# Idle products at the start, small loads on ScalarE's queue, and a last batch in three units

## The reference

```python
x = x + (x @ W.T + (x @ A0[label]) @ B0.T * 0.5)         # layer 0, rank 32
x = x + quantise(x, thresholds, deltas, zero_points)     # layer 1, 8 levels of scale
x = x + x @ W2[adapter].T                                # layer 2, weights of 1024 x 1024 per batch
x = x + (x @ B3[adapter].T) @ A3[adapter].T              # layer 3, rank 16
```

## Time and profile before

| | |
|---|---|
| median of 3 runs | 486.47 us (485.25 to 486.58) |
| the profiled execution: its time, its span | 486.57 us, 484.8 us |
| TensorE, matmul records: busy | 462.4 us, 95% |
| VectorE: busy | 427.1 us, 88% |
| ScalarE: busy | 315.0 us, 65% |
| mean granted TensorE clock | 0.988 |

### The profile page before, as it was taken

The page is one execution under the profiler, slowest core; times in us unless marked ns, Lnnn a source line. Parts: engine busy times, 40 slices in busy tenths (PEclk is TensorE's granted clock), DMA queues, the critical chain, the costliest instruction groups (busy, mean ns, idle before and its releaser), DMA issues.

```text
span 484.8 us, 7178 instructions
## 1 busy us (share of the span) xinstructions
PE 462.4 (95%) x2944; PEld 424.8 (88%) x2944; DVE 427.1 (88%) x389; ACT 315.0 (65%) x237; POOL 11.0 (2%) x16
## 2 busy tenths in 40 slices
PE   3998997999999999999999999999999999997995
PEld 3998996889998899989998999989998899884883
DVE  3589999999899977999599997999869996899953
ACT  4489979955696529956297635986269641966600
POOL 0001000000000000000000000000000010000000
PEclk9999999899999999999999999999999999997999
DMA  7883030264025442073323642135123332246022
GB/s 254 315 315 99 3 99 0 87 235 160 12 78 187 171 126 87 1 272 110 103 89 126 233 124 88 39 136 175 39 87 122 139 126 88 87 166 221 0 88 87
DMA packets 17461, 60.25 MB, mean 124 GB/s; under 512 B 2964, under 2 KB 5012, under 8 KB 13332
## 3 DMA queue, kind: packets, MB, share of 16 engines
q1 hardware_dynamic: 17428, 59.79, 35.9%
HBM read 51.39 MB, written 8.39 MB: 123 GB/s over the span
## 4 chain that ended last, share of the span: by engine, by line
PE 74%; DVE 15%; issue 6%; ACT 3%; DMA 1%; SPq 0%; DVEq 0%; ACTq 0%
PE l_ps L759 32%; PE l_ps L708 28%; PE l_ps L774 6%; DVE quant L578 5%; DVE cand L552 3%; PE bx_ps L791 3%; PE bx_ps L730 2%; PE l_ps L804 1%; DVE quant L572 1%; DMA x_raw<-x 1%; ACT cand L391 1%; DVE x_lo L505 1%; DVE cand L560 1%; PE l_ps L718 1%; DVE w_lo L487 1%
## 5 line engine op out<-in xcount | busy, mean ns | idle before, releaser
L759 PE MATMUL l_ps<-x,w_sb 128*128 128x256 f32 x896 | 197.4, 382 | 2.3 <-DVE x L632 2.0
L759 PEld LDWEIGHTS l_ps<-x,w_sb 128*128 128x128 f32 x896 | 170.6, 192 | 25.8 <-issue 2.9
L578 DVE COPY_PREDICATED quant<-mask,cand 128x2048 f32<-128x2048 int8 (+3 forms) x70 | 143.9, 2055 | 12.0 <-ACT mask L401 7.1
L401 ACT ACTIVATE mask<-magnitude,thr_bias 128x2048 fp8e5<-128x2048 f32 (+3 forms) x70 | 115.8, 1655 | 38.2 <-DVE quant L578 38.0
L391 ACT ACTIVATE cand<-x,inv_delta 128x2048 f32<-128x2048 f32 (+3 forms) x80 | 132.1, 1652 | 4.5 <-DVE quant L572 1.8
L552 DVE TENSOR_SCALAR cand<-cand,delta 128x2048 f32<-128x2048 f32 (+3 forms) x80 | 86.2, 1077 | 12.2 <-ACT cand L391 12.0
L708 PE MATMUL l_ps<-x_hi,w_hi 128*128 128x256 f32 x512 | 86.0, 291 | 9.7 <-ACT w_hi L325 7.4
L560 DVE TENSOR_SCALAR cand<-cand,lower,upper 128x2048 f32<-128x2048 f32 (+3 forms) x80 | 91.3, 1142 | 0.4
L708 PE MATMUL l_ps<-x_lo,w_hi 128*128 128x256 f32 x512 | 83.8, 287 | 0.0
L708 PE MATMUL l_ps<-x_hi,w_lo 128*128 128x256 f32 x512 | 83.7, 286 | 0.0
L708 PEld LDWEIGHTS l_ps<-x_hi,w_hi 128*128 128x128 f32 x512 | 72.2, 195 | 12.8 <-ACT w_hi L325 7.4
(11 more groups left out here) (52 smaller groups left out, 234.8 us busy)
## 6 DMA issues: line engine op xcount, KB each, us to landing
w_sb<-w SPq DMA_DIRECT2D x31, 1024.0 KB, 5.1
out<-x SPq DMA_DIRECT2D x32, 256.0 KB, 2.2
x_raw<-x SPq DMA_DIRECT2D x15, 512.0 KB, 5.7
w_sb<-w SPq DMA_DIRECT2D x7, 512.0 KB, 6.2
a_raw<-a SPq DMA_DIRECT2D x48, 64.0 KB, 4.4
a_raw<-a SPq DMA_DIRECT2D x8, 128.0 KB, 4.6
x<-w SPq DMA_DIRECT2D x1, 1024.0 KB, 5.6
x_raw<-x SPq DMA_DIRECT2D x2, 256.0 KB, 4.7
```

The source lines that it names most:

```text
L401: act.activation(mask[:, m % MASKS, 0:n], magnitude[:, 0:n], ACT.Relu, bias=thr_bias[:, k:k + 1], scale=STEEP, saturate=False).then_inc(ma ...
L578: dve.copy_predicated(y, mask[:, m % MASKS, 0:n].bitcast(I8), t).then_inc(merged, 1)
L759: last = nc.tensor.matmul(l2_bank(b, q)[:, i * S:(i + 1) * S], w2_tile(b, o)[:, k * P:(k + 1) * P], x2[:, b % SLOTS, k * S:(k + 1) * S], s ...
```

## The change

The change does three things. TensorE runs 24 products of the identity with itself, `WARM`, before its first tile, into a bank that is not yet in use. ScalarE's queue issues the loads of both id vectors and of the three parameter vectors, ahead of its other work; SyncE issues tile 3 before B0, and the orders in which ScalarE and VectorE split the weights are written out anew: ScalarE splits tiles 4 and 5 before the low-rank product's high part, and VectorE computes the parameters between `add_diag(4)` and `add_diag(5)` instead of after all splits. The last batch has three units, of blocks 0 to 3, 4 and 5, 6 and 7; the work between their steps, the parts of `last_layer2` and the place of `split_bx(B - 2)` change with them.

```diff
-LAST_SPLIT = 5
+PARTS = (0, 4, 6, 8)
+WARM = 24
 UNITS = ((0, 0, HW), (0, HW, HW)) + tuple((b, 0, BW) for b in range(1, B - 1))\
-    + ((B - 1, 0, LAST_SPLIT * S), (B - 1, LAST_SPLIT * S, BW - LAST_SPLIT * S))
+    + tuple((B - 1, first * S, (end - first) * S) for first, end in zip(PARTS, PARTS[1:]))
+LAST = len(UNITS) - len(PARTS) + 1
...
 SyncE
-            sp.dma_start(label_ids[:, :], ...)
-            sp.dma_start(adapter_ids[:, :], ...)
             load_w0(1)
             load_w0(2)
             sp.wait_ge(ids_loaded, 2 * 16)
             load_a0(0)
+            load_w0(3)
             for q in range(4):
                 sp.dma_start(a3_raw[q * QUAD:(q + 1) * QUAD, :], b0).then_inc(b0_loaded, 16)
-            (three parameter loads)
-            for n in range(3, T):
+            for n in range(4, T):
                 load_w0(n)
...
 ScalarE, between(u, j)
-                    if j == 7:
+                    if j == 7 and s + 1 < B - 1:
                         drain_l0(s + 1, 1)
-                elif u == len(UNITS) - 2:
+                elif u == LAST:
                     if j == 2:
                         split_a3(s - 1)
-                else:
-                    if j == 1:
-                        split_bx(s - 1)
+                    if j == 3:
+                        drain_l0(s, 1)
 ScalarE, main
+            (five small loads, then as before)
             split_w0(1)
+            split_w0(2)
             split_a0(0)
-            split_w0(2)
+            split_w0(3)
             act.wait_ge(b0_loaded, 4 * 16)
             act.activation(b0_split[:, :], a3_raw[:, :], ACT.Copy, scale=0.5).then_inc(b0_hi_done, 1)
-            for n in range(3, T):
-                if n == 4:
-                    low_rank_hi(0)
-                split_w0(n)
+            split_w0(4)
+            split_w0(5)
+            low_rank_hi(0)
+            split_w0(6)
+            split_w0(7)
+            act.wait_ge(param_step, 6)
             drain_l0(0, 0)
-            act.wait_ge(param_step, 6)
             for u in range(len(UNITS)):
                 quantise(u)
+            split_bx(B - 2)
             split_a3(B - 1)
             split_bx(B - 1)
...
 VectorE, between(u, j)
-                elif u == len(UNITS) - 2:
+                elif u == LAST:
                     if j == 2:
                         split_a3(s - 1)
-                    if j in (1, 3, 5, 7):
-                        drain_l2(s - 1, j // 2)
-                else:
-                    if j == 1:
-                        split_bx(s - 1)
+                    if j == 6:
+                        drain_l2(s - 1, 0)
+                elif u == LAST + 1:
+                    if j in (0, 3, 6):
+                        drain_l2(s - 1, j // 3 + 1)
 VectorE, main: the order after is
   add_diag(1) split_x(0, 1) add_diag(2) split_w0(1) split_w0(2) add_diag(3) split_a0(0)
   split_w0(3) (B0) add_diag(4) (parameters) add_diag(5) split_w0(4) low_rank_lo(0)
   add_diag(6) split_w0(5) add_diag(7) split_w0(6) split_w0(7), all units, split_bx(B - 2), finish ...
 TensorE
-            def last_layer2(half):
+            def last_layer2(part):
-                pe.wait_ge(x2_done, x2_count(b) - 1 + half)
+                pe.wait_ge(x2_done, LAST + part + 1)
...
-                        for k in (range(LAST_SPLIT), range(LAST_SPLIT, T))[half]:
+                        for k in range(PARTS[part], PARTS[part + 1]):
...
+            pe.wait_ge(ident_ready, 1)
+            for i in range(WARM):
+                nc.tensor.matmul(l3_ps[:, 0:P], ident[:, :], ident[:, :], start=True, stop=True)
...
             for q in range(4):
                 layer2(B - 2, q)
+            last_layer2(0)
             for q in range(4):
                 low_rank3(B - 2, q)
-            last_layer2(0)
+            last_layer2(1)
             for q in range(4):
                 layer3(B - 2, q)
-            last_layer2(1)
+            last_layer2(2)
```

More of the change, by code:

```diff
@@ L644, in _ @@
             split_first_w0(1)
+            add_diag(1)
             split_x(0, 1)
[L646 removed]
+            add_diag(2)
             split_w0(1)
+            split_w0(2)
+            add_diag(3)
             split_a0(0)
[L649 to L650 removed]
+            split_w0(3)
             rows = slice(QUAD, 2 * QUAD)
@@ L654, in _ @@
                                      b0_split[rows, :].bitcast(F32), ALU.mult, ALU.subtract).then_inc(b0_split_done, 1)
-            add_diag(3)
-            for n in range(3, T):
-                if n + 1 < T:
-                    add_diag(n + 1)
-                if n == 4:
-                    low_rank_lo(0)
-                split_w0(n)
+            add_diag(4)
             dve.wait_ge(params_loaded, 3 * 16)
@@ L670, in _ @@
             dve.tensor_scalar(thr_bias[:, :], sorted_thr[:, :], -STEEP, None, ALU.mult).then_inc(param_step, 1)
+            add_diag(5)
+            split_w0(4)
+            low_rank_lo(0)
+            add_diag(6)
+            split_w0(5)
+            add_diag(7)
+            split_w0(6)
+            split_w0(7)
             dve.wait_ge(param_step, 6)
@@ L761, in layer2 @@
                 last.then_inc(l2_done, 1)
-            def last_layer2(half):
+            def last_layer2(part):
                 b = B - 1
-                if half == 0:
+                if part == 0:
                     pe.wait_ge(x0_done, 2 * B)
-                pe.wait_ge(x2_done, x2_count(b) - 1 + half)
+                pe.wait_ge(x2_done, LAST + part + 1)
                 for q in range(4):
-                    if half == 0:
+                    if part == 0:
                         pe.wait_ge(w2_loaded[q], (b + 1) * 16)
@@ L777, in last_layer2 @@
                                                     start=(i == 0 and k == 0), stop=(i == 1 and k == T - 1))
-                    if half == 1:
+                    if part == len(PARTS) - 2:
                         last.then_inc(l2_done, 1)
```

14 lines of the change are left out of this document (6 added, 8 removed).

## The result

| | before | after |
|---|---|---|
| median (lowest to highest), beside each other | 485.11 us (484.32 to 486.58) | 488.21 us (487.56 to 489.73) |
| ratio of the times, 95% interval | | 1.0064 [1.0048, 1.0081] |
| profiled execution: time, span, granted clock | 486.57, 484.8, 0.988 | 489.59, 487.8, 0.980 |
| first candidate | 29.78 | 29.70 |
| layer 2 of batch 0 starts | 83.28 | 83.21 |

Forecast were 484.2 us and a range of 482.4 to 487.4; 488.21 lies outside it. Both profiled executions are some 1.4 us above their medians, so their difference, 3.0 us of span, can stand for that of the medians, 3.1. Its parts are the differences of the table's rows: nothing at the head (−0.07 where −3.9 was forecast), 1.26 us between 83 and 411, and 1.84 in the tail (1.6 was forecast; 66.77 against 64.93 us).

A forecast was written before the change was run, and what follows sets the result against it. TensorE was taken to bound most of the span, with VectorE bounding quantisation at the head. Head −3.9 us and tail +1.6 us make −2.3, so 486.5 becomes 484.2 us, range 482.4 to 487.4.

The forecast's parts named there:

- The step that failed: Head: tile 1 stays near 9.95 and tile 2 near 11.35; small packets sharing the DMA engines cost x 0.3 us.
- my bound of 0.6 us: Head: upper end of the 0 to 0.6 us allowed for small packets sharing the DMA engines with x.
- my first rival: Head: clock falls again between the first twelve products and 11.8, gap 0.4 to 2 us; 485.8 us, chance 0.2.
- The head's gain of 3.9 us: Head: first candidate starts at 25.9 instead of 29.78, 3.9 us sooner; bounds 0.5 and 4.3.
- the forecast chain of steps: TensorE's next products from 11.8, low-rank product done about 21.1, first candidate 25.9, layer 2 of batch 0 at 79.4.
- The idle products: TensorE's start: 24 products from 1.5 us, 0.12 us a record, twice that at low clock, ending between 8.3 and 10.3.
- The overrun: Rival: idle products' records exceed about 0.2 us warm, real tiles begin at 15 to 17; 486.5 to 488 us, chance 0.13.
- The stage from 83 to 411: TensorE-bound batches after quantisation: layer 2 starts at 79.4 instead of 83.28, the head's 3.9 us passing through.
- The tail: Batch 6's layer 2 onward: TensorE stands 5.4 us for the later drain, low clock costs 2.5; 1.6 us slower (0.8 to 2.5).
- the rival in which only the tail counts: Head's gain lost between 25 and 83 us to a wait now just covered, 5.4 us stall stays; 488 us, chance 0.12.
- the sum of −2.3 us: Whole kernel: head −3.9 and tail +1.6, taken from 486.5 to give 484.2 us.

The follow-up runs named there:

- parameters early on SyncE: Changed kernel with the three parameter loads on SyncE right behind x's second half, ahead of tile 1, ids staying on ScalarE; 487.44 us, ratio 1.0038 to before.
- ids on ScalarE: Changed kernel with only the three parameter loads back on SyncE behind B0, both id loads staying on ScalarE; 484.43 us, ratio 0.9972 to before.
- a mended head: Changed kernel with all five small loads on SyncE, ids after x's second half, parameters after B0, new tail kept; 484.63 us, ratio 0.9996 to before.
- The head measured alone: Kernel before with the change's head only, all small loads on SyncE, last batch in two units as before; 482.57 us, ratio 0.9944 to before.

## Why the prediction was wrong, point by point

**The step that failed** is the one on the landings: tiles 1 and 2 "both stay about there", and "the small packets share the DMA engines with x; I take 0.3 us for them, from 0 to 0.6 us". Measured, x's second half came 2.8 us later (11.45 against 8.7), tile 1 2.9 and tile 2 3.9. I had priced the small packets by the engine time that they occupied in the earlier trace rows, 1.16 of the engines for half a microsecond, "in which most of them moved". That reading was wrong. In before the three loads were issued at 11.52, 11.98 and 12.46 and landed 2.5, 2.6 and 3.3 us later, at 14.0, 14.6 and 15.8, and the windows just ahead of the one that I had taken show the engines nearly idle:

```profile
13.00:13.50 0.50, 1.00 0.29 55
13.50:14.00 0.50, 1.00 0.11 7
14.00:14.50 0.50, 1.00 0.40 45
```

Tile 3 had been issued at 12.93, right behind them. A part of this quiet may be tile 3's own start; with the parameters early on SyncE it is not, since tile 1 had been issued 2.7 us before the engines went quiet. So what small packets cost here is the time in which nothing else moves, and not only the time that they occupy. On one queue that is already above my bound of 0.6 us: 1.1 us at the candidate and 1.5 us of nearly idle engines with the parameters early on SyncE. What a second queue adds, no row of before could show. The kernel with all five on SyncE shows that the landings, and nothing else in the new head, lost the gain: one edit, and x's half is at 8.69, tile 1 at 9.94, the candidate at 26.05. The same loads on the kernel before, and nothing else, make 3.1 us.

The Trainium skill ("DMA: Bandwidth & Descriptors", Issuing engines are not separate DMA queues) says that loads issued by different engines interleave on the same 16 DMA engines, and that several issuers save issue time only. The runs agree as far as they go: with the small loads on the second queue x came 2.8 us later. No run has them on the one queue ahead of x. How much small packets on one can slow large loads on the other that section does not say.

**From there the loss is arithmetic.** TensorE's products begin at 14.42 instead of 11.8, 2.6 us, and behind 3.1 us of standing the clock was low, as in my first rival, whose gap of "0.4 to 2 us" had become 3.1: the products up to about 17 ran at 0.215 us a record. The fall was not bound to come, and it did not set the candidate alone. With the parameters early on SyncE TensorE stood 3.0 us in the same place and went on at 0.12 us a record. And in after the copies of tiles 4 and 5 ended at the same time as the low-rank product; in the two other kernels with this head ScalarE waited 0.3 and 1.15 us for it. The low-rank copy is at 25.16 where 21.1 to 21.6 was forecast, the candidate at 29.70 where it was 25.9. The head's gain of 3.9 us is 0.07. Where the landings are right, the forecast chain of steps (11.8, 21.1, 25.9, 79.4) is met within a few tenths: 11.88, 21.26, 25.81 and 79.45 with the ids on ScalarE.

**The idle products** were costed right: forecast end between 8.3 and 10.3, measured 9.9. A record was forecast at 0.12 us and at twice that at the low clock, and seven run in the window of 1.5 to 3.0 us, 0.21 each, and sixteen in that of 7.5 to 9.0, some 0.1 each: that is nearer the lower bound of 0.107 than the 0.12 taken. The weight load is hidden. The overrun, a rival at 0.13, did not come.

**The stage from 83 to 411** was forecast to move whole. It grew by 1.26 us, because the clock behind the stand of 2.0 us was low for longer (96 records in 23.90 us, before 22.64). "Even if that fall goes away, its 1.9 us are hardly won" proved right: with all small loads on SyncE there was no fall, and TensorE waited 1.4 us for the first drain instead. From layer 2 of batch 0 to the next batch's takes 58.5 us in that kernel and in before, and 59.7 in after. A short fall is covered by VectorE and costs nothing; a long one is not, and costs 1.2.

**The tail** was right in mechanism and size. The stall is 5.0 us, forecast 5.4; the drain begins 18.2 us after layer 2 of batch 6, forecast 18.6; clock 3.1 us, forecast 2.5 of 1.7 to 3.4; the whole stretch 66.77, forecast 66.5. The experiments agree within their intervals: the old tail under the same head is 2 us faster, the new one under a mended head 2.5 us slower than the old. In single executions the size depends on how soon the clock is back: this stretch takes 65.2 to 66.8 us in the seven kernels with the late drains, and 64.3 to 65.0 in the four with the old tail. A step of 512 columns takes 1.47 us, estimated at 1.45.

**The chances.** The result came out at the number of the rival in which only the tail counts (488, chance 0.12), and its mechanism, a "first transfer delayed by small packets", is what happened, though it bit ahead of 25 us and not between 25 and 83, where I had put it. A chance of 0.12 was too low for a cost whose row was taken from another queue. That the number fits as well is luck: 488 was 486.5 plus the tail's 1.6 us, the kernel before stood at 485.11 beside the new one, and of the 3.1 us between them 1.26 are the longer fall of the clock, which I had not forecast.

With the landings mended the sum of −2.3 us (a ratio of 0.9953) stands against 0.9972 [0.9953, 0.9991] with the ids on ScalarE and 0.9996 [0.9976, 1.0016] with all on SyncE. So even there the forecast was too good by 0.9 and 2.1 us; the first interval just reaches it, the second does not. The head measured alone gives 2.7 us (1.7 to 3.8) of the 3.9, and the tail takes 2 to 2.5 where 1.6 was forecast.

## What to carry to other kernels

A load is not free because it is small: three loads of 4 KB in 432 small packets on a second queue, beside the first large loads, delayed those by 2.8 us and cost the kernel 3.1; in this kernel they belong behind the large ones that the start waits for, on the same queue. Their price is read from the time in which the engines move nothing else, and a cost taken from a row with one queue is no bound for two. A drain that frees a bank is placed by when TensorE comes back for it: five microseconds of standing cost eight here (6.6 where the clock was back sooner), because the clock falls behind the stand, and two steps earlier it costs nothing. Keeping the clock high at the start is worth what waits for TensorE there, and only if the data come before it stands again.

## What the runs showed of the hardware

**Small packets leave the engines partly idle, on one queue and on two.** With the parameters' 32-byte packets ahead of tile 1 on the one queue, the share is 0.16 and the rate 28 GB/s for 1.5 us. In 4 to 8 us the rate is 216 GB/s at a share of 0.66 with the parameters on the second queue, and 389 at 1.02 with all on one. When the second queue starts late, its own 4 KB loads take 8.4 to 10.7 us; on the one queue they took between 2.5 and 7.8. Why the engines stand while large loads are waiting is open. The one-queue kernel shows that it needs no second queue; whether the larger delay with two comes from the turns between queues or from the place ahead of x, no run here tells.

**The clock falls for different lengths after the same stand.** Layer 2 of batch 0 always follows a stand of 2.0 us. Two kernels show no fall behind it (all on SyncE; ids on ScalarE), before and four others a short one (first 96 records 22.64 us), after and seven others a longer one (23.80 to 23.93). Here is the kernel with all small loads on SyncE, and then after, in windows of TensorE:

```profile
82.00:84.00 2.00, 2.00 (x11) 1.00 0.00 0
84.00:86.00 2.00, 2.00 (x11) 1.00 0.00 0
```

```profile
83.00:84.00 1.00, 0.79 (x2) 0.50 0.00 0
...
88.00:89.00 1.00, 1.00 (x4) 0.50 0.00 0
89.00:90.00 1.00, 1.00 (x6) 0.91 0.00 0
```

The tail's stall shows it too: the 64 records behind it take 15.5 and 15.7 us in two kernels and 16.7 to 17.0 in the five others that have it. Each of the two makes 1.1 to 1.6 us, where single executions of one kernel differ by 0.7 to 4.5 us here; that the one causes the other is likely, since profiled executions alone show the clock, but not shown. What decides the length, or whether there is a fall at all, was not found: in the head a stand of 3.0 us was followed by none in one kernel, and stands of 2.9, 3.1 and 3.6 us by a low clock in three.

**The granted clock reads 1.00 at the very start whatever the rate.** In after the column says 1.00 for 1.5 to 3.0 us, where the idle products' records take 0.21 us, and for 7.5 to 9.0, where they take some 0.1. From the first fall on (0.50 in 15 to 16) it agrees with the pitch. Until the column has shown its first fall, the distance between starts is the measure, and not the column.

**Without idle products the clock rises at different times.** Two kernels without idle products have the same twelve records from 7.14 and 7.16 us on. In one, 0.12 us a record is reached at 11.5, behind a stand of 1.3 us, in the other only at about 16, behind one of 1.8. In before, too, it was at about 16, behind a stand of only 0.7, so the length of the stand does not decide it. In all eleven kernels with the idle products it was high by 8.5; that is what they buy, a start that no longer depends on this.
